# The products of probabilities and latents of a batch in one run, behind the value-output weights' product

## The chip, the cores and the metric

One core of a Trainium2 chip. The time is that of the device in microseconds, as the median of several executions. Engines: TensorE (PE, with its weight loads as PEld), VectorE (DVE), ScalarE (ACT), GpSimd (POOL), SyncE (SP), which here only issues transfers.

## What is computed

One layer on x of shape (2, 512, 512), all in fp32: latent attention with 32 heads, then a feed-forward part with low-rank corrections.

```python
def _mla_forward(hidden_states, Wq_a, q_a_ln_w, Wq_b, Wkv_a, kv_a_ln_w, Wkv_b, Wo):
    q = _rmsnorm(hidden_states @ Wq_a, q_a_ln_w) @ Wq_b        # rank 192, 32 heads of 128 + 64
    q_nope, q_pe = (q[..., :NOPE], q[..., NOPE:])
    ckv = hidden_states @ Wkv_a
    compressed, k_pe = (ckv[..., :KV_RANK], ckv[..., KV_RANK:])  # rank 64, rotary 64
    kv = _rmsnorm(compressed, kv_a_ln_w) @ Wkv_b
    k_nope, v = (kv[..., :NOPE], kv[..., NOPE:])
    ...  # rotary embedding of q_pe and k_pe
    scores = jnp.einsum('bhqd,bhkd->bhqk', qf, kf) * scale
    scores = jnp.where(causal, scores, jnp.finfo(scores.dtype).min)
    probs = jax.nn.softmax(scores, axis=-1)
    o = jnp.einsum('bhqk,bhkd->bhqd', probs, v)
    return o @ Wo

x = x + _layernorm(_L0_attn_ref(_layernorm(x)))
x = x + _layernorm(_L0_ffn_ref(_layernorm(x)))
```

## The kernel before

The kernel works with the latents themselves. It folds the key half of Wkv_b into the query weights, and the value half into Wo, so that a head's output is first probabilities times the 64 normalised latents, and later one product with the folded weights. Four stages follow each other: latents of all tokens (to about 45 us), the attention loop over 16 pairs of heads (to about 465 us), the output projection, and the feed-forward part. The change is in the attention loop.

One body of the loop serves one pair of heads, p, in 16 units k: k = 0 to 7 are the first batch (in counts, number 2p, the even one), k = 8 to 15 the second (number 2p + 1, the odd one); within a batch, k // 4 % 2 is the head and i = k % 4 the block of 128 query rows, which by the causal mask has i + 1 blocks of keys. So units have 128, 256, 384, 512 columns in turn. Body 0 and body 15 are written out (`first`, `last`), the 14 between are a loop. There are no planner and no priorities: the order of each engine's queue is the order of the source in its own `body`, and semaphore waits tie the queues together.

For one unit the work goes round the engines:
- TensorE, `scores`, two units ahead (in unit k it makes the scores of unit k + 2): three fp32r products into bank k % 2. It waits until VectorE has read the same bank two units before (`a.s_masked`, U - 1).
- VectorE, `mask_and_max`, also two units ahead: adds the mask, scales, takes the row extreme (line 635).
- ScalarE, `exponent`, two units ahead: exp and its sum (line 367).
- TensorE, `turn_p`, last in unit k: turns the probabilities of unit k (line 1002), after `a.exp_made`.
- ScalarE, `move_p`, first in unit k: copies them from the bank to `pt` (line 375).

Around this, TensorE's body has other work at fixed units, each ahead of that unit's `turn_p`:
- `absorb_query(p + 1)` at k = 0, the query weights of the next pair, into bank XB (5); it needs the transfer `sq`.
- `output(2p - 1, ...)` at k = 1, 2, 3: probabilities times latents of the odd batch of the pair before, for j = 0, then 1, then 2 and 3 (j is the block of keys; the columns are 512 - 128 j). `output(2p, ...)` at k = 9 (j = 0) and k = 10 (j = 1, 2, 3). Each j is two products, one per head, with 64 output columns, in the two column halves of the array (line 1014). They add up in bank 4 and wait until all eight units of their batch are in `pt`.
- `absorb_output(p)` at k = 8: the value-output weights of this pair, two products of 64 output columns and 512 columns (line 1032), into bank XB. ScalarE copies them to `vs` at its k = 9 (line 446), and SP stores them to device memory.
- `turn_r(2p - 1)` at k = 4 and `turn_r(2p)` at k = 11: the reciprocals of the sums, turned, into bank XB (line 1024). The second waits for ScalarE's copy of the weights (`a.wvo_moved`), since both use the bank. ScalarE copies them to `rsb` (`move_r`, line 383) at k = 5 and 12, and VectorE scales the output with them (`scale_o`, line 648) at k = 6 and 13.
- `query` at k = 5, 7, 13, 15: the rotated and absorbed queries, five fp32r products of 512 columns each, into banks 6 and 7. VectorE rotates them (`rotate_swapped`, `rotate_own`), GpSimd adds the halves, ScalarE rounds them (`query_hi`, line 357, at k = 2, 4, 10, 12), VectorE takes the rest (`query_lo`, line 625).

Bank XB thus serves, in turn, the query weights, the odd batch's reciprocals, the value-output weights and the even batch's reciprocals, and each user waits for the reader of the one before.

SP's loop for pair p: wait `wq_split`, load `sq`; wait `wvo_made`, load `sv`; wait `wvo_moved`, store `vs`. The load of `sq` of a pair stands behind the store of the pair before.

In body 15 there are no queries; at k = 11 to 15 pieces of the output projection (`project`) stand in their place, and ScalarE and VectorE split the folded weights.

Of the kernel before, what the change touches and what calls it, by code (L numbers as in the profile page):

```python
# [30 lines left out]
QB = SEQ // P  # L31
# [44 lines left out]
def build(nc, x_d, wa_d, lnw_d, cst_d, kcs_d, sq_d, sv_d, w13_d, bs_d, a13_d, a2_d, w2_d, b2_d, out_d):  # L76
# [137 lines left out]
    with block:  # L214
# [120 lines left out]
        def _(act):  # L335
# [80 lines left out]
            def body(p, first=False, last=False):  # L416
                for k in range(PU):
                    if last and k == 6:
                        split_output(0, 0)
                    if last and k in (13, 14):  # L420
                        if k == 13:
                            act.wait_ge(a.o_made, 2 * PAIRS - 1)
                        split_weights(k - 7)
                    move_p(PU * p + k, k, 2 * p - 1 + k // UNITS if k % UNITS == 0 and not first else None)
                    n = k + 2
                    if n < PU:
                        exponent(PU * p + n, n, first and n < 4, 2 * p if n == UNITS and not first else None)
                    elif not last:
                        exponent(PU * p + n, n - PU, False, 2 * p + 1 if n == PU else None)
                    if k == (3 if first else 1) and not last:  # L430
                        weights_hi(p + 1)
                    if k in (2, 4):
                        h = (k - 2) // 2
                        query_hi(4 * p + 2 + h, 1, h, None if first else PU * (p - 1) + UNITS + QB * (h + 1))
                    if k in (10, 12) and not last:
                        h = (k - 10) // 2
                        query_hi(4 * p + 4 + h, 0, h, PU * p + QB * (h + 1))
                    if k == 5 and not first:
                        move_r(2 * p - 1)
                    if k == 12:  # L440
                        move_r(2 * p, first)
                    if k == 9:
                        act.wait_ge(a.wvo_made, p + 1)
                        if not first:
                            act.wait_ge(a.wvo_out, 16 * p)
                        nc.scalar.activation(vs[:, :], bank[XB][:, :], ACT.Copy).then_inc(a.wvo_moved, 1)
# [149 lines left out]
        def _(dve):  # L596
# [83 lines left out]
            def body(p, first=False, last=False):  # L680
                for k in range(PU):
                    n = k + 2
                    if n < PU or not last:
                        mask_and_max(PU * p + n, n % PU)
                    if last and k == 7:
                        split_output(0, 0)
                    if last and k >= 8:
                        split_weights(k - 8)
                    if k == (4 if first else 2) and not last:
                        weights_lo(p + 1)  # L690

                    b, r, gi = (1, k, 4 * p + 2) if k < UNITS else (0, k - UNITS, 4 * p + 4)
                    if k < UNITS or not last:
                        if first and k in (1, 2):
                            rotate_swapped(gi + k - 1, k - 1)
                            if k == 1:
                                rotate_own(gi, 0)
                        elif first and k == 3:
                            rotate_own(gi + 1, 1)
                        elif r == 1:  # L700
                            rotate_swapped(gi + 1, 1)
                        elif r in (0, 2) and not (first and k == 0):
                            rotate_own(gi + r // 2, r // 2)
                        if r in (3, 5):
                            query_lo(gi + r // 2 - 1, b, r // 2 - 1)
                        if r == 7 and not last:
                            rotate_swapped(gi + 2, 0)
                    if k == 6 and not first:
                        scale_o(2 * p - 1, p - 1, 1)
                    if k == 13:  # L710
                        scale_o(2 * p, p, 0)
                    if k == 7:
                        invert(2 * p, 0, first)
                    if k == 15:
                        invert(2 * p + 1, 1)
# [242 lines left out]
        def _(pe):  # L958
# [17 lines left out]
            def query(gi, b, h, w=None, first=False):  # L976

                if w is not None:
                    pe.wait_ge(a.wq_split, w + 1)
                if not first:  # L980
                    pe.wait_ge(a.q_rotated, gi - 1)
                out, tok = bank[6 + h][:, :], slice(b * SEQ, (b + 1) * SEQ)
                three(out, w1_hi[:, h, :], w1_lo[:, h, :], ql_hi[:, 0, tok], ql_lo[:, 0, tok], True, False)
                nc.tensor.matmul(out, w2[:, h, :], ql_hi[:, 1, tok], start=False, stop=False)  # L984
                nc.tensor.matmul(out, w2[:, h, :], ql_lo[:, 1, tok], start=False, stop=True).then_inc(a.q_made, 1)  # L985
# [20 lines left out]
            def output(m, b, js, first=False):  # L1006

                if 0 in js:
                    pe.wait_ge(a.p_moved, UNITS * (m + 1))
                    if not first:  # L1010
                        pe.wait_ge(a.o_scaled, m)
                for j in js:
                    for h in range(2):
                        last = nc.tensor.matmul(bank[4][RKV * h:RKV * (h + 1), j * P:SEQ], kvn[:, QB * b + j, 0:RKV],  # L1014
                                                pt[:, b, h, j, j * P:SEQ], start=(j == 0), stop=(j == QB - 1),
                                                skip_group_check=True)
                if QB - 1 in js:
                    last.then_inc(a.o_made, 1)
# [34 lines left out]
            def body(p, first=False, last=False):  # L1053
                for k in range(PU):
                    n = k + 2
                    if n < PU:
                        scores(PU * p + n, n, 4 * p + n // QB)
                    elif not last:
                        scores(PU * p + n, n - PU, 4 * p + 4)
                    if k == (2 if first else 0) and not last:  # L1060
                        if first:
                            pe.wait_ge(f.qk_split, TB - 1)
                        else:
                            pe.wait_ge(a.r_moved, 2 * p - 1)
                        absorb_query(p + 1)
                    if k == 1 and not first:
                        output(2 * p - 1, 1, [0])
                    if k == 2 and not first:
                        output(2 * p - 1, 1, [1])
                    if k == 3 and not first:  # L1070
                        output(2 * p - 1, 1, [2, 3])
                    if k == 4 and not first:
                        if last:
                            pe.wait_ge(a.r_moved, 2 * p - 1)
                        else:
                            pe.wait_ge(a.wq_split, p + 2)
                        turn_r(2 * p - 1)
                    if k == 8:
                        if first:
                            pe.wait_ge(a.wq_split, p + 2)  # L1080
                        else:
                            pe.wait_ge(a.r_moved, 2 * p)
                        absorb_output(p)
                    if k in (5, 7) and not last:
                        query(4 * p + 4 + k // 7, 0, k // 7, p + 1)
                    if k == 9:
                        output(2 * p, 0, [0], first)
                    if k == 10:
                        output(2 * p, 0, [1, 2, 3])
                    if last and k in (11, 12, 13, 14, 15):  # L1090
                        project(0, 0, {11: (0,), 12: (1,), 13: (2,), 14: (3, 4), 15: (5,)}[k])
                    if k == 11:
                        pe.wait_ge(a.wvo_moved, p + 1)
                        turn_r(2 * p)
                    if k in (13, 15) and not last:
                        query(4 * p + 6 + k // 15, 1, k // 15)
                    turn_p(PU * p + k, k, first and k < 2)
                    if first and k < 2:
                        if k == 0:
                            pe.wait_ge(f.qk_split, TB)  # L1100
                        query(2 + k, 1, k)
# [211 lines left out]
```

## Time and profile before

| what | value |
|---|---|
| time, median of 3 (lowest, highest) | 654.0 us (653.73, 654.58) |
| profiled execution: span of the instructions | 652.1 us |
| the same execution's own time | not given apart; the median above is 1.9 us over the span |
| busy TensorE / VectorE / ScalarE / GpSimd | 607.9 / 529.2 / 412.8 / 166.0 us |
| granted TensorE clock, mean | 0.984 of full speed |

An engine's share is its busy time over the span. The end of a matmul is modelled, so on TensorE the distance from one start to the next says more than the duration of a row. A row `x3` merges three instructions; `[0.17 <-ACT pr L367]` says that the engine stood idle 0.17 us before it, until ScalarE's line 367 was done. In a row of fp32 products one product is two instructions.

### The profile page before, as it was taken

The page shows a single profiled execution, that of the slowest core. Times are in us where ns is not written, and L with a number is a line of the kernel's source. Part 1 is how long each engine was busy: PE and PEld are TensorE (multiplying, and loading weights), DVE is VectorE, ACT ScalarE, POOL GpSimd, SP SyncE. Part 2 cuts the span into 40 slices and gives each one's busy share as a digit, 9 for nine tenths or more (in the row PEclk, how much of TensorE's full clock was granted, in tenths as well). Part 3 has the DMA queues.
Part 4 walks back from the last instruction along what each step waited for, and adds up shares of the span by engine and source line. Part 5 has one row for each costly group of instructions (what it writes and reads, how often), then busy time and mean ns, then how long its engine had stood idle before and what let it go on. Part 6 is the DMA issues. An engine that isn't in the chain of part 4 may idle for free.

```text
span 652.1 us, 12397 instructions
## 1 busy us (share of the span) xinstructions
PE 607.9 (93%) x3432; PEld 448.6 (69%) x3432; DVE 529.2 (81%) x1292; ACT 412.8 (63%) x1157; POOL 166.0 (25%) x137
## 2 busy tenths in 40 slices
PE   5778999999999999999999999999999878789996
PEld 4666667767777776677677777766787656666664
DVE  4987788888888888888888888889877888886456
ACT  4455777878777777778787777777733333155343
POOL 2011222122213212221222132121043333125520
PEclk9998999999999999999999999999999998979999
DMA  8000211201202202112012022022760000001003
GB/s 320 16 1 1 82 39 43 80 25 56 80 0 80 65 15 80 36 44 80 19 61 80 0 80 64 17 93 80 234 235 1 0 1 1 28 2 49 0 16 114
DMA packets 13862, 37.80 MB, mean 58 GB/s; under 512 B 1328, under 2 KB 1584, under 8 KB 13584
## 3 DMA queue, kind: packets, MB, share of 16 engines
q1 hardware_dynamic: 13840, 37.53, 17.3%
q8 instruction: 11, 0.18, 0.1%
q14 instruction: 11, 0.09, 0.0%
HBM read 31.24 MB, written 6.29 MB: 58 GB/s over the span
## 4 chain that ended last, share of the span: by engine, by line
PE 71%; DVE 18%; ACT 4%; issue 3%; DMA 3%; SPq 0%; DVEq 0%; ACTq 0%
PE bank L1002 13%; PE bank L1014 12%; PE bank L961 11%; PE bank L962 11%; PE bank L963 11%; DVE dot L833 6%; PE bank L1032 2%; PE bank L1024 2%; PE bank L971 2%; PE bank L985 2%; PE bank L984 2%; DMA x<-x 2%; PE bank L1181 2%; DVE st L809 2%; DVE ss L635 1%
## 5 line engine op out<-in xcount | busy, mean ns | idle before, releaser
L367 ACT ACTIVATE pr<-ss,small 128x128 f32<-128x128 f32 (+3 forms) x256 | 143.2, 559 | 41.4 <-DVE small L635 40.8
L375 ACT ACTIVATE pt<-bank 128x128 f32<-128x128 f32 (+3 forms) x256 | 110.9, 433 | 61.3 <-PE bank L1002 61.1
L635 DVE CUSTOM_DVE_ANT_0 ss<-bank,cst 128x128 f32<-128x128 f32 (+3 forms) x256 | 123.3, 486 | 14.0 <-PE bank L963 9.6
L1002 PE MATMUL bank<-ident,pr 128*128 128x128 f32 x640 | 119.0, 284 | 3.1 <-ACT pr L367 2.9
L1002 PEld LDWEIGHTS bank<-ident,pr 128*128 128x128 f32 x640 | 75.6, 142 | 66.6 <-ACT pr L367 34.0
L284 POOL TENSOR_TENSOR qrot<-qrot,qswp 64x512 f32<-64x512 f32 x64 | 82.8, 1294 | 138.5 <-DVE qrot L621 138.5
L961 PE MATMUL bank<-kt_hi,qt_hi 128*128 128x128 f32 (+3 forms) x256 | 101.0, 394 | 3.6 <-DVE qt_lo L625 2.7
L1014 PE MATMUL bank<-pt,kvn 128*64 128x256 f32 (+3 forms) x512 | 86.2, 448 | 0.7 <-ACT pt L375 0.7
L963 PE MATMUL bank<-kt_hi,qt_lo 128*128 128x128 f32 (+3 forms) x256 | 83.2, 325 | 0.0
L962 PE MATMUL bank<-kt_lo,qt_hi 128*128 128x128 f32 (+3 forms) x256 | 83.0, 324 | 0.0
L625 DVE TENSOR_TENSOR qt_lo<-qrot,qt_hi 128x512 fp32r<-128x512 f32 x64 | 60.3, 942 | 24.7 <-ACT qt_hi L357 24.5
L294 POOL COPY rb<-small 128x512 f32<-128x512 f32 x32 | 19.8, 617 | 212.8 <-DVE small L643 212.8
L961 PE MATMUL bank<-wv,o_s 128*128 128x512 f32 x128 | 52.5, 410 | 10.0 <-POOL o_s L318 10.0
L961 PEld LDWEIGHTS bank<-kt_hi,qt_hi 128*128 128x128 f32 x256 | 49.9, 195 | 6.1 <-DVE qt_lo L625 2.9
L962 PE MATMUL bank<-wv,o_s 128*128 128x512 f32 x128 | 51.2, 400 | 0.0
L963 PE MATMUL bank<-wv,o_s 128*128 128x512 f32 x128 | 51.1, 399 | 0.0
L963 PEld LDWEIGHTS bank<-kt_hi,qt_lo 128*128 128x128 f32 x256 | 48.8, 191 | 2.7
L962 PEld LDWEIGHTS bank<-kt_lo,qt_hi 128*128 128x128 f32 x256 | 49.4, 193 | 0.1
L367 ACT ACTIVATION_READ_ACCUMULATOR pr<-ss,small 128x1 f32 x256 | 49.2, 192 | 0.0
L1014 PEld LDWEIGHTS bank<-pt,kvn 128*64 128x64 f32 x512 | 29.9, 135 | 27.8 <-ACT pt L375 11.6
L318 POOL TENSOR_TENSOR o_s<-ot,o_s 128x1024 fp32r<-128x1024 f32 x13 | 32.7, 2522 | 61.2 <-ACT o_s L397 61.2
L615 DVE TENSOR_TENSOR qswp<-bank,cst 32x512 f32<-32x512 f32 x64 | 44.5, 695 | 2.0
(168 smaller groups left out, 1179.7 us busy)
## 6 DMA issues: line engine op xcount, KB each, us to landing
sv<-sv SPq DMA_DIRECT2D x16, 576.0 KB, 3.7
sq<-sq SPq DMA_DIRECT2D x16, 448.0 KB, 3.5
wvo_scratch<-vs SPq DMA_DIRECT2D x16, 256.0 KB, 2.1
wv_raw<-wvo_scratch SPq DMA_DIRECT2D x8, 512.0 KB, 4.2
xa<-x SPq DMA_DIRECT2D x8, 256.0 KB, 5.5
x<-x SPq DMA_DIRECT2D x1, 2048.0 KB, 10.9
out<-yo SPq DMA_DIRECT2D x8, 256.0 KB, 2.0
w<-w SPq DMA_DIRECT2D x1, 1376.0 KB, 14.1
```

The source lines that it names most:

```text
L284: nc.gpsimd.tensor_tensor(qrot[RKV:P, h, :], qrot[RKV:P, h, :], qswp[RKV:P, h, :], ALU.add)\
L367: nc.scalar.activation(pr[:, k % 4, 0:n], ss[:, k % 2, 0:n], ACT.Exp, bias=negmax[:, k % 8:k % 8 + 1], scale=-1.0, accum_out=rsum[:, k:k + ...
L375: nc.scalar.activation(pt[:, b, h, 0:i + 1, i * P:(i + 1) * P], bank[2 + k % 2][:, 0:(i + 1) * P].rearrange("p (j q) -> p j q", q=P), ACT. ...
L615: nc.vector.tensor_tensor(qswp[64:96, h, :], G[96:128, :], sin1[96:128, :], ALU.mult)
L625: nc.vector.tensor_tensor(qt_lo[:, b, h, :], qrot[:, h, :], qt_hi[:, b, h, :].bitcast(F32), ALU.subtract)\
L635: nc.vector.tensor_tensor_reduce(out=ss[:, k % 2, 0:n], in0=bank[k % 2][:, 0:n], in1=mask[:, SEQ - n:SEQ], scale=-SCALE, scalar=3.4e38, op ...
L833: nc.vector.tensor_tensor_reduce(out=dot[:, j % 2, :], in0=xn2[:, :], in1=a13[:, j, :], scale=1.0, scalar=0.0, op0=ALU.mult, op1=ALU.add, ...
L961: nc.tensor.matmul(out, w_hi, x_hi, start=start, stop=False)
L962: nc.tensor.matmul(out, w_hi, x_lo, start=False, stop=False)
L963: return nc.tensor.matmul(out, w_lo, x_hi, start=False, stop=stop)
L1002: last = nc.tensor.transpose(bank[2 + k % 2][:, j * P:(j + 1) * P], pr[:, k % 4, j * P:(j + 1) * P], ident[:, :])
L1014: last = nc.tensor.matmul(bank[4][RKV * h:RKV * (h + 1), j * P:SEQ], kvn[:, QB * b + j, 0:RKV], pt[:, b, h, j, j * P:SEQ], start=(j == 0), ...
```

## The change

- The three pieces of `output` of the odd batch (k = 1, 2, 3) become one at k = 2.
- `absorb_output(p)` moves from k = 8 to k = 10, and right behind it all four j of `output(2p)` follow, so far at k = 9 and 10.
- `turn_r(2p)` moves from k = 11 to k = 12.
- ScalarE's copy of the value-output weights moves from k = 9 to k = 11, its copy of the even batch's reciprocals from k = 12 to k = 13; VectorE's scaling of that batch from k = 13 to k = 14.

Semaphores and their counts stay as they are.

```diff
@@ scalar engine, body @@
-                    if k == 12:
+                    if k == 13:
                         move_r(2 * p, first)
-                    if k == 9:
+                    if k == 11:
                         act.wait_ge(a.wvo_made, p + 1)
                         if not first:
                             act.wait_ge(a.wvo_out, 16 * p)
@@ vector engine, body @@
-                    if k == 13:
+                    if k == 14:
                         scale_o(2 * p, p, 0)
@@ tensor engine, body @@
-                    if k == 1 and not first:
-                        output(2 * p - 1, 1, [0])
                     if k == 2 and not first:
-                        output(2 * p - 1, 1, [1])
-                    if k == 3 and not first:
-                        output(2 * p - 1, 1, [2, 3])
+                        output(2 * p - 1, 1, range(QB))
...
-                    if k == 8:
+                    if k in (5, 7) and not last:
+                        query(4 * p + 4 + k // 7, 0, k // 7, p + 1)
+                    if k == 10:
                         if first:
                             pe.wait_ge(a.wq_split, p + 2)
                         else:
                             pe.wait_ge(a.r_moved, 2 * p)
                         absorb_output(p)
-                    if k in (5, 7) and not last:
-                        query(4 * p + 4 + k // 7, 0, k // 7, p + 1)
-                    if k == 9:
-                        output(2 * p, 0, [0], first)
-                    if k == 10:
-                        output(2 * p, 0, [1, 2, 3])
+                        output(2 * p, 0, range(QB), first)
...
-                    if k == 11:
+                    if k == 12:
                         pe.wait_ge(a.wvo_moved, p + 1)
                         turn_r(2 * p)
```

## Rows read from the trace of the kernel before

**Rows 1.** The page, part 1: busy us (share of the span) xinstructions.

```profile
PE 607.9 (93%) x3432; PEld 448.6 (69%) x3432; DVE 529.2 (81%) x1292; ACT 412.8 (63%) x1157; POOL 166.0 (25%) x137
```

**Rows 2.** Stretches: length; busy PE, PEld, DVE, ACT, POOL; granted clock; DMA share; GB/s.

```profile
44.00:80.00 36.00, 31.24 (x174) 24.36 (x174) 26.99 (x79) 22.11 (x68) 8.36 (x7) 0.91 0.12 38
...
257.56:283.22 25.66, 25.49 (x163) 18.53 (x162) 22.03 (x57) 19.60 (x59) 6.37 (x6) 1.00 0.17 51
```

**Rows 3.** Timeline, TensorE, that body: start us, us, engine, line, operation, count.

```profile
259.35 0.40 PE L962 MATMUL bank<-kt_lo,qt_hi 128*128 128x512 f32 x1
259.59 0.40 PE L963 MATMUL bank<-kt_hi,qt_lo 128*128 128x512 f32 x1
259.91 1.08 PE L1014 MATMUL bank<-pt,kvn 128*64 128x512 f32 x4
260.92 0.44 PE L1002 MATMUL bank<-ident,pr 128*128 128x128 f32 x2
...
268.37 0.55 PE L1002 MATMUL bank<-ident,pr 128*128 128x128 f32 x3 [0.17 <-ACT pr L367]
...
271.31 1.08 PE L1032 MATMUL bank<-sv 128*64 128x512 f32 x4
...
273.28 1.08 PE L1014 MATMUL bank<-pt,kvn 128*64 128x512 f32 x4
...
274.48 0.30 PE L961 MATMUL bank<-kt_hi,qt_hi 128*128 128x128 f32 x1
...
274.94 1.52 PE L1014 MATMUL bank<-pt,kvn 128*64 128x384 f32 x12
276.39 0.55 PE L1002 MATMUL bank<-ident,pr 128*128 128x128 f32 x3
...
277.14 0.60 PE L1024 MATMUL bank<-ident,rb 128*128 128x128 f32 x4
277.58 0.60 PE L1002 MATMUL bank<-ident,pr 128*128 128x128 f32 x4
277.93 0.43 PE L961 MATMUL bank<-kt_hi,qt_hi 128*128 128x384 f32 x1
...
278.58 0.47 PE L961 MATMUL bank<-kt_hi,qt_hi 128*128 128x512 f32 x1
...
283.22 0.42 PE L961 MATMUL bank<-kt_hi,qt_hi 128*128 128x384 f32 x1
```

**Rows 4.** Timeline of VectorE in the same body.

```profile
270.46 0.69 DVE L648 TENSOR_TENSOR ot<-bank,rsb 128x512 f32 x1 [0.69 <-ACT rsb L383]
...
273.17 0.56 DVE L635 CUSTOM_DVE_ANT_0 ss<-bank,cst 128x384 f32<-128x384 f32 x1
```

**Rows 5.** Timeline of ScalarE in the same body.

```profile
268.13 0.19 ACT L367 ACTIVATION_READ_ACCUMULATOR pr<-ss,small 128x1 f32 x1
...
275.75 0.59 ACT L446 ACTIVATE vs<-bank 128x512 f32<-128x512 f32 x1
276.98 0.49 ACT L375 ACTIVATE pt<-bank 128x384 f32<-128x384 f32 x1 [0.64 <-PE bank L1002]
277.36 0.39 ACT L367 ACTIVATE pr<-ss,small 128x128 f32<-128x128 f32 x1
...
277.75 0.62 ACT L357 ACTIVATE qt_hi<-qrot 128x512 fp32r<-128x512 f32 x1
278.27 0.59 ACT L375 ACTIVATE pt<-bank 128x512 f32<-128x512 f32 x1
278.75 0.50 ACT L367 ACTIVATE pr<-ss,small 128x256 f32<-128x256 f32 x1
```

**Rows 6.** Timeline of SP in the same body, and landing of the sq loads.

```profile
276.50 0.35 SPq L235 DMA_DIRECT2D wvo_scratch<-vs  x1
277.38 0.33 SPq L231 DMA_DIRECT2D sq<-sq  x1
...
DMA to landing us min/median/max: 3.2/3.5/5.8
```

## The prediction

> **What bounds the kernel now.** First the busy time by engine: TensorE 93% of the span, VectorE 81%, ScalarE 63% [rows 1]. Such shares are averages, so next one pair of heads by itself: a steady body of the loop lasts 25.66 us, TensorE is busy for 25.49 of it at full clock, VectorE for 22.03 and ScalarE for 19.60 [rows 2]. TensorE looks like the only bound, but VectorE has only 3.6 us in hand and ScalarE 6.1, and the three engines feed one another every second unit. So the third view is the timeline of TensorE, and the question in each row is whether it starts where the row before lets it or where another engine does. In this body nearly all starts are TensorE's own. The exception is turning the probabilities of unit 6, at 268.37, which waits for exp(6): ScalarE's read of its sum ends at 268.32 [rows 3, 5]. TensorE therefore runs just ahead of a VectorE and ScalarE chain that is nearly as long as its own. That makes it necessary to walk the change through all three queues instead of adding up TensorE's savings. I write unit k for one row block of a body, turn(k) for turning its probabilities, mask(k) for VectorE's pass over its scores.
>
> **What the change takes from TensorE.** The products with 64 output columns stand in six runs per body now: three for the odd batch (units 1, 2, 3), one for the value-output weights (unit 8), two for the even batch (units 9, 10). The run of one 512-column pair takes 1.01 us from its start to the next instruction (259.91 to 260.92), that of 384, 256 and 128 columns, 768 in all, 1.45 us (274.94 to 276.39) [rows 3]. So 256 more columns cost 0.44 us, 512 columns 0.88, and 0.13 us of each run is not columns: leaving the run. Entering costs some more: score products of 512 columns follow each other at 0.24 (259.35 to 259.59), and the run starts 0.32 after the last (259.91); so 0.08 us. A run costs about 0.21 us beyond its columns by this, 0.24 if leaving is 0.16 as I take below for the longest one; I take 0.24. After the change there are two runs, so TensorE has 4 x 0.24 = 0.96 us less to do per body.
>
> The Trainium skill (TensorEngine Tiling, section Tiling Modes, Key Properties) says that changing the tiling mode, not merely the tile, drains TensorE. The trace agrees that going in and out costs time that the columns don't. By that rule alone the change is a gain; the rival that takes it so is the first below.
>
> **First half of a body (odd batch), units 0 to 6.** Two runs fewer: -0.48 us for TensorE. But turn(6) already waits for exp(6), and this comes behind mask(6) [rows 3, 5]: TensorE's gain ends there unless VectorE and ScalarE move too. They gain a little (turn(1) now comes 1 us sooner, and ScalarE's copies behind it), and lose a little: VectorE's scaling of the even batch's output moves one unit later, past the mask of the next body's unit 0, and now waits for a copy that ScalarE makes a unit later, so mask(2) is late for scores(4), by my estimate some 0.3 us (half of one such scaling, 0.69 in rows 4). Bounds -0.5 and +0.4; I take 0, since the row is one of waiting already.
>
> **Second half, from turn(6).** Here the moves matter.
> 1. scores(12) may not start before mask(10), which reads the same bank, is done. mask(10) ends at 273.17 + 0.56 = 273.73, which is 5.36 us after turn(6) [rows 3, 4]. VectorE can't do it sooner: its work before it is the even-batch rotation of the next body, and ahead of that the scaling at 270.46, which had idled 0.69 us for ScalarE's copy of the reciprocals, which hangs on exp(6) like turn(6) itself. TensorE now reaches scores(12) at 274.48, 6.11 us after turn(6), so 0.75 us to spare. But 2 x 1.01 = 2.02 us of what keeps it busy until then, the weights' product at 271.31 and the first even-batch product at 273.28, moves behind scores(12). TensorE comes at 6.11 - 2.02 = 4.09 and waits until 5.36 + 0.07 (semaphore; ScalarE's to TensorE took 0.05, rows 3 and 5) = 5.43. Wait 1.3 us; scores(12) is 0.68 us earlier than now.
> 2. From scores(12) to turn(10) it is 1.91 us now (274.48 to 276.39) [rows 3]. Two groups of 512 columns are added inside the one run, 2 x 0.855 (0.88 by the slope, 0.85 if leaving costs 0.16, since 1.01 - 0.16 = 0.85): +1.71 us.
> 3. The turning of the reciprocals (unit 11 now, at 277.14; unit 12 then) may not overwrite its bank before ScalarE has copied the weights' product, and this copy moves from unit 9 to unit 11. In ScalarE's queue it stands behind moving turn(10) (0.59 after turn(10)'s start: 276.39 to 276.98), exp(12), the rounded query copy, moving turn(11) and exp(13). Their starts are 276.98, 277.36, 277.75, 278.27, 278.75, and the next thing starts 0.49 after the last: 279.24. That is 2.85 us after turn(10); the copy itself takes 0.59 (275.75), ends at +3.44, and with 0.05 TensorE goes on at +3.49 [rows 5]. What TensorE has to do until then: turn(10) and scores(13), 0.75 (276.39 to 277.14), turn(11), 0.35 (277.58 to 277.93), scores(14), 0.61 (277.93 to 278.58, less 0.04 that I give to turn(12), one block): 1.7 us [rows 3]. It waits 1.8 us. Then 0.44 for the reciprocals (277.14 to 277.58) and 0.04 for turn(12), and scores(15) starts at +3.97. Now it starts at 278.58 - 276.39 = +2.19. So +1.78 us. Behind the waiting instruction on TensorE stand turn(12), scores(15) and the query products; VectorE's mask(15) and ScalarE's moves wait for them. Without the query copy in ScalarE's way (if it got done sooner) the wait would be 1.3 us; that is its lower bound.
> 4. From scores(15) to the next body's scores(2) is 4.64 us (278.58 to 283.22) [rows 3], TensorE's own work; nothing in it changes but the place of ScalarE's copy of the reciprocals (unit 13), which still ends before the next body's query weights need the bank. I take 0.
>
> Sum per body: 0 - 0.68 + 1.71 + 1.78 = **+2.81 us**, a body of about 28.5 us. It holds 1.3 + 1.8 us of new waiting, against 0.96 us of TensorE work saved.
>
> SP's queue is moved too: the store of the weights' product follows ScalarE's copy (0.88 us ahead of the load of the query weights, 276.50 and 277.38), and these land 3.5 us later in the median [rows 6]. Copy end to landing is some 0.2 + 0.9 + 3.5 = 4.6 us; after that copy's end TensorE needs 0.5 + 4.64 + 0.6 = 5.7 us to where it uses them. About 1 us of cover is left; the slowest load (5.8) would cost 1.2 us in a body. Counted as nothing, kept for the upper end. The load of the value weights is issued when their product is done, a whole body ahead: nothing.
>
> **The whole.** Fourteen bodies are like this one: 14 x 2.81 = 39.3 us. Body 0 has only the second half, its VectorE has one scaling less and its TensorE ran slower before it [rows 2], so the mask wait may be smaller: +2 (1.5 to 2.8). In the last body products of the output projection at units 11 and 12 cover 1.4 us of the wait for the copy, and there are no queries: +1 (-0.5 to 2). Sum +42.3 us. On the profiled execution: span 652.1 to 694.4. Its time is not shown apart from its span; the three runs have the median 654.0, 1.9 us above it, and with that the forecast is 654.0 + 42.3 = **696.3 us**.
>
> **Rivals.**
> - TensorE stays the bound (the other side): the waits don't come, and the saving does: 14 x 0.96 + 0.5 + 1.0 = 15 us, 639. It decides if mask(10) comes 1.3 us sooner after turn(6) and the copy 1.8 us sooner. For it: TensorE's 25.49 of 25.66 us busy. Against it: both are in-order queues whose rows stand back to back, and the last is a copy behind five instructions, two of them waiting for TensorE's own turn(11) or turn(10).
> - Only the wait for the copy comes: VectorE, its masks being ready sooner, gets ahead, and scores(12) starts when TensorE arrives. Then +2.81 - 1.33 = 1.48 per body, 14 x 1.48 + 2 = 23 us: 677. Against: the 0.69 us that VectorE idled for ScalarE's copy.
> - The clock falls as well. In the stretch from 44 to 80 us, where TensorE was busy for 31.24 of 36.00, the granted clock was 0.91 against 1.00 in the steady bodies [rows 2]. A share of 0.18 of 36 us at the lower of the two levels (1.2 GHz) is 6.5 us, a loss of 3.2. Half of that per body would be 14 x 1.6 = 23 us more: 719. For it: TensorE would be busy for some 25.4 of 28.5 us, 0.89, little above the 0.87 there. Against: that stretch still begins in the first stage, whose waits are many, while here two waits of under 2 us lie some 6 us apart.
> - The change doesn't do what it says: the 0.24 us is not a cost of a run but of the first product after another kind, and stays. In the second half the waits hide it, so it shows only as some 0.25 us per body: 700.
>
> **Chances.** Forecast 0.72, TensorE stays the bound 0.05, copy wait alone 0.10, clock 0.08, no saving 0.05. The range: from the copy wait alone with a first half at its lower bound, (1.48 - 0.1) x 14 + 2 = 21, to the forecast with half of the clock's loss and late loads, +62: 674 to 716. Measured differences under 0.2% (1.3 us) count as the same: faster 0.06, same 0.02, slower 0.92.
>
> **What would show it.** In a steady body: two runs of 64-column products, the second 3.2 us long; TensorE idle 1.3 us before scores(12), put down to VectorE's mask, and 1.8 us before the turning of the reciprocals, put down to ScalarE's copy; bodies 28.5 us apart; VectorE's busy time per body unchanged at 22. Wrong, if bodies stand at 25.7 us or less, if the waits are there but at other places, or if the granted clock in the steady bodies is under 1.00.

## The result and the profile after

The changed kernel takes **695.0 us** (694.0 to 696.1), the kernel before 653.9 in the same comparison: a ratio of 1.063, 95% interval 1.061 to 1.066. The forecast was 696.3 us. The profiled execution took 694.56 us, its span is 692.8 us, 40.7 more than before.

The page, part 1, of the changed kernel, as in [rows 1]:

```profile
PE 605.9 (87%) x3432; PEld 456.9 (66%) x3432; DVE 523.8 (76%) x1292; ACT 410.4 (59%) x1157; POOL 165.5 (24%) x137
```

TensorE's busy time, whose ends are modelled, fell by 2.0 us while the span grew by 40.7: the time is waiting. One steady body, from turn(6) to the next turn(6) (length; busy PE, PEld, DVE, ACT, POOL; granted clock; DMA share; GB/s), against [rows 2]:

```profile
259.66:288.05 28.39, 25.38 (x160) 19.10 (x161) 21.63 (x56) 19.45 (x60) 6.35 (x6) 1.00 0.14 46
```

28.39 us in place of 25.66, TensorE busy for 25.38 of it, at full clock. The timeline of TensorE in it (start, duration, engine, line, operation, count, idle time before and what ended it), against [rows 3]:

```profile
259.66 0.55 PE L1002 MATMUL bank<-ident,pr 128*128 128x128 f32 x3 [0.16 <-ACT pr L367]
...
262.51 0.27 PE L1002 MATMUL bank<-ident,pr 128*128 128x128 f32 x1
262.84 0.50 PE L961 MATMUL bank<-kt_hi,qt_hi 128*128 128x512 f32 x1
...
263.63 0.38 PE L1002 MATMUL bank<-ident,pr 128*128 128x128 f32 x2
265.08 0.33 PE L961 MATMUL bank<-kt_hi,qt_hi 128*128 128x128 f32 x1 [1.07 <-DVE small L635]
...
265.56 1.08 PE L1032 MATMUL bank<-sv 128*64 128x512 f32 x4
266.47 2.33 PE L1014 MATMUL bank<-pt,kvn 128*64 128x512 f32 x16
268.73 0.55 PE L1002 MATMUL bank<-ident,pr 128*128 128x128 f32 x3
...
269.83 0.42 PE L961 MATMUL bank<-kt_hi,qt_hi 128*128 128x384 f32 x1
...
272.21 0.66 PE L1024 MATMUL bank<-ident,rb 128*128 128x128 f32 x4 [1.60 <-ACT vs L446]
...
272.73 0.48 PE L961 MATMUL bank<-kt_hi,qt_hi 128*128 128x512 f32 x1
...
277.36 0.42 PE L961 MATMUL bank<-kt_hi,qt_hi 128*128 128x384 f32 x1
...
279.63 0.38 PE L1002 MATMUL bank<-ident,pr 128*128 128x128 f32 x2
280.12 0.33 PE L961 MATMUL bank<-kt_hi,qt_hi 128*128 128x128 f32 x1
...
280.60 2.38 PE L1014 MATMUL bank<-pt,kvn 128*64 128x512 f32 x16
282.91 0.55 PE L1002 MATMUL bank<-ident,pr 128*128 128x128 f32 x3
...
288.05 0.55 PE L1002 MATMUL bank<-ident,pr 128*128 128x128 f32 x3 [0.17 <-ACT pr L367]
```

Two waits stand there that [rows 3] has not: 1.07 us before scores(12) (265.08), ended by VectorE's mask, and 1.60 us before the turning of the reciprocals (272.21), ended by ScalarE's copy into `vs`. The idle time named is counted from the modelled end of the row before; from start to start the waits are longer: turn(9), two blocks, begins at 263.63 and would be through at 263.77, so 1.31 us are lost. Counted like that, turn(6) waits 0.3 us as before, and there are short waits that carry no mark. The turning of one block ahead of scores(11) takes 0.33 us (262.51 to 262.84) where 0.03 to 0.08 is usual, and that of two blocks ahead of scores(4) takes 0.49 (279.63 to 280.12) where 0.14 is usual. Each of these two scores starts 0.06 to 0.07 us after the mask that reads its bank: mask(9) and mask(2) below. A shorter one, 0.1 to 0.2 us, stands before scores(7).

All in all TensorE waits some 4.3 us in this body, against some 0.5 in the body before. What is left, 24.1 us and 25.2, is also what bodies with two and with six runs take where TensorE waits for nothing (experiments 10 and 5). So the change did save 1.1 us of TensorE's work, where 0.96 was forecast.

What the waits hang on, first VectorE (mask(9), mask(10), and the scaling of the even batch behind mask(0) of the next body, with mask(2) after it), against [rows 4]:

```profile
262.36 0.41 DVE L635 CUSTOM_DVE_ANT_0 ss<-bank,cst 128x256 f32<-128x256 f32 x1
...
264.46 0.56 DVE L635 CUSTOM_DVE_ANT_0 ss<-bank,cst 128x384 f32<-128x384 f32 x1
...
275.63 0.29 DVE L635 CUSTOM_DVE_ANT_0 ss<-bank,cst 128x128 f32<-128x128 f32 x1 [0.44 <-PE bank L963]
...
276.79 0.69 DVE L648 TENSOR_TENSOR ot<-bank,rsb 128x512 f32 x1 [0.86 <-ACT rsb L383]
...
279.50 0.56 DVE L635 CUSTOM_DVE_ANT_0 ss<-bank,cst 128x384 f32<-128x384 f32 x1
```

then ScalarE, against [rows 5]:

```profile
269.31 0.49 ACT L375 ACTIVATE pt<-bank 128x384 f32<-128x384 f32 x1 [2.22 <-PE bank L1002]
269.69 0.39 ACT L367 ACTIVATE pr<-ss,small 128x128 f32<-128x128 f32 x1
...
270.08 0.62 ACT L357 ACTIVATE qt_hi<-qrot 128x512 fp32r<-128x512 f32 x1
270.60 0.58 ACT L375 ACTIVATE pt<-bank 128x512 f32<-128x512 f32 x1
271.08 0.50 ACT L367 ACTIVATE pr<-ss,small 128x256 f32<-128x256 f32 x1
...
271.57 0.59 ACT L446 ACTIVATE vs<-bank 128x512 f32<-128x512 f32 x1
```

The same five pieces stand ahead of the copy, with the same distances as in [rows 5] (0.38, 0.39, 0.52, 0.48, 0.49), and ScalarE idled 2.22 us before the first of them: it had nothing to do while TensorE was in the long run, and had everything to do after it.

### The profile page after: what moved, and what is told of

Read it like the earlier page. It is cut to its first block, busy times and chain, and to the rows that moved or that the text cites. A ratio compares the mean times of both kernels' runs of the same rounds, so it can differ in the third digit from the quotient of the medians.

```text
span 692.8 us, 12397 instructions
## 1 busy us (share of the span) xinstructions
PE 605.9 (87%) x3432; PEld 456.9 (66%) x3432; DVE 523.8 (76%) x1292; ACT 410.4 (59%) x1157; POOL 165.5 (24%) x137
## 4 chain that ended last, share of the span: by engine, by line
PE 53%; DVE 20%; issue 12%; ACT 10%; DMA 2%; DVEq 1%; SPq 0%; ACTq 0%
PE bank L1014 10%; PE bank L961 10%; PE bank L963 8%; PE bank L962 8%; PE bank L1002 6%; DVE dot L833 6%; ACT pr L367 3%; PE bank L1024 3%; PE bank L1032 2%; DVE ss L635 2%; ACT pt L375 2%; DMA x<-x 2%; DVE st L809 1%; PE bank L1174 1%; ACT rsb L383 1%
## 5 line engine op out<-in xcount | busy, mean ns | idle before, releaser
L1002 PE MATMUL bank<-ident,pr 128*128 128x128 f32 x640 | 115.6, 279 | 4.2 <-ACT pr L367 4.0
L1002 PEld LDWEIGHTS bank<-ident,pr 128*128 128x128 f32 x640 | 78.5, 142 | 26.6 <-ACT pr L367 8.0
L1014 PE MATMUL bank<-pt,kvn 128*64 128x256 f32 (+3 forms) x512 | 75.2, 436 | 0.7 <-ACT pt L375 0.7
L625 DVE TENSOR_TENSOR qt_lo<-qrot,qt_hi 128x512 fp32r<-128x512 f32 x64 | 57.7, 902 | 17.1 <-ACT qt_hi L357 17.1
L1014 PEld LDWEIGHTS bank<-pt,kvn 128*64 128x64 f32 x512 | 35.4, 137 | 45.5 <-issue 34.3
L961 PE MATMUL bank<-wv,o_s 128*128 128x512 f32 x128 | 53.8, 420 | 6.7 <-POOL o_s L318 6.7
L962 PE MATMUL bank<-wv,o_s 128*128 128x512 f32 x128 | 52.3, 408 | 0.0
L963 PE MATMUL bank<-wv,o_s 128*128 128x512 f32 x128 | 52.1, 407 | 0.0
```

The source lines that it names most:

```text
L625: nc.vector.tensor_tensor(qt_lo[:, b, h, :], qrot[:, h, :], qt_hi[:, b, h, :].bitcast(F32), ALU.subtract)\
L961: nc.tensor.matmul(out, w_hi, x_hi, start=start, stop=False)
L962: nc.tensor.matmul(out, w_hi, x_lo, start=False, stop=False)
L963: return nc.tensor.matmul(out, w_lo, x_hi, start=False, stop=stop)
L1002: last = nc.tensor.transpose(bank[2 + k % 2][:, j * P:(j + 1) * P], pr[:, k % 4, j * P:(j + 1) * P], ident[:, :])
```

## The experiments

All are timed beside the kernel before on the same chip; a body is measured from turn(6) to turn(6), or between two equal places, in the steady loop. In the diffs `...` stands for lines left out, and the comments after `#` are added here.

**1. The copy first in unit 10** (the run stays in unit 10).

```diff
+                    if k == 10:   # scalar engine, ahead of move_p(10)
+                        act.wait_ge(a.wvo_made, p + 1)
...
-                    if k == 11:
-                        act.wait_ge(a.wvo_made, p + 1)
```

> The changed kernel (695.0 us), with one edit: ScalarE copies the value-output weights' product first thing in unit 10, ahead of moving turn(10), not last in unit 11; everything else stays, so the single run is still at unit 10 behind scores(12). My theory: the 1.8 us per body in which TensorE waits for this copy go, since the copy is then ready before TensorE gets there, and nothing else is late in its place; TensorE's turning of the reciprocals comes 1.75 us sooner after turn(10), the wait before scores(12) stays at 1.1 to 1.3 us: 16 x 1.75 = 28 us less at most, about 669 us (665 to 674), steady body 26.6 us. Rival, that the copy wait only covers a chain of VectorE and ScalarE that is as long: less than half of it comes back, the time stays over 682 us.

667.2 us (ratio 1.021, 1.018 to 1.023): 27.8 us came back, as the theory had it, and the body is 26.57 us (turn(6) at 247.00 and 273.57). The wait before scores(12) stayed as it was, so the copy's wait was not cover for another:

```profile
247.00 0.55 PE L1002 MATMUL bank<-ident,pr 128*128 128x128 f32 x3 [0.16 <-ACT pr L367]
...
252.43 0.33 PE L961 MATMUL bank<-kt_hi,qt_hi 128*128 128x128 f32 x1 [1.06 <-DVE small L635]
...
273.57 0.55 PE L1002 MATMUL bank<-ident,pr 128*128 128x128 f32 x3 [0.17 <-ACT pr L367]
```

**2. The run in unit 9**, ahead of scores(12), copy and the rest late as in the changed kernel.

```diff
-                    if k == 10:
+                    if k == 9:
                         if first:
                             pe.wait_ge(a.wq_split, p + 2)
```

> The changed kernel (695.0 us), with one edit on TensorE: the run (weights' product and all products of the even batch) stands in unit 9, ahead of scores(12), not in unit 10 behind it. Copies, turning of reciprocals and scaling stay at their late units. My theory: the wait for mask(10) goes (TensorE is busy for 3.2 us while VectorE gets there), and the wait for the copy stays, 1.3 us or somewhat more: scores(15) at 11.7 us after turn(6) against 13.0 in the changed kernel, so 1.3 to 1.5 us per body less: about 674 us (669 to 679). Rival, that TensorE waits for VectorE's masks wherever the run stands: the wait moves to the next scores and the time stays over 688 us.

681.6 us (1.042, 1.040 to 1.045), outside the 669 to 679 expected; a body of 27.43 (turn(6) at 254.20 and 281.63): 0.96 us shorter than the changed kernel's, where I expected 1.3 to 1.5. The mask wait of 1.31 us is gone as expected; the miss is ScalarE. The run now stands ahead of turn(9) and not behind it, so ScalarE has one unit more to make up for when it ends, exp(11) of 512 columns among it. TensorE's turn(11) waits for that, 0.34 us from start to start, which is the difference between 1.31 and 0.96; and then the copy's wait is as long as before. This is read from the trace; no run moved exp(11) by itself:

```profile
285.70 1.08 PE L1032 MATMUL bank<-sv 128*64 128x512 f32 x4
...
290.48 0.66 PE L1002 MATMUL bank<-ident,pr 128*128 128x128 f32 x4 [0.17 <-ACT pr L367]
...
293.22 0.66 PE L1024 MATMUL bank<-ident,rb 128*128 128x128 f32 x4 [1.57 <-ACT vs L446]
```

**3. Both repairs, the reciprocals at their old units.** The run in unit 9, the copy first in unit 9, `turn_r`, `move_r`, `scale_o` of the even batch at 11, 12, 13.

```diff
-                    if k == 11:   # scalar engine: the copy; now ahead of move_p(9)
+                    if k == 9:
...
-                    if k == 10:   # tensor engine: absorb_output and output
+                    if k == 9:
...
-                    if k == 12:   # turn_r; move_r 13 -> 12, scale_o 14 -> 13
+                    if k == 11:
```

> Both repairs together: one run in unit 9, ScalarE's copy of the weights' product first thing in unit 9, and the turning of the reciprocals, their copy and the scaling at the units of the kernel before (11, 12, 13); the odd batch's products in one run in unit 2 as in the changed kernel. My theory: no new wait is left and the four runs saved are worth what TensorE can use of them, -0.3 to -0.9 us per body against the kernel before: 640 to 650 us, most likely 647. Rival 1, that the waits were not the cause but the long run itself: over 660 us. Rival 2, that entering and leaving a run costs nothing: 653 to 655 us.

646.0 us (0.989, 0.987 to 0.991): 1% faster than the kernel before, within the range of 640 to 650. The two long waits were the cause of the loss, and the long run by itself is not.

**4. The odd batch alone**, the kernel before with one run in unit 2.

```diff
-                    if k == 1 and not first:
-                        output(2 * p - 1, 1, [0])
                     if k == 2 and not first:
-                        output(2 * p - 1, 1, [1])
-                    if k == 3 and not first:
-                        output(2 * p - 1, 1, [2, 3])
+                        output(2 * p - 1, 1, range(QB))
```

> The kernel before (653.9 us), with only the first part of the change: the odd batch's three pieces in one run in unit 2; all of the even batch as before. TensorE has 2 x 0.24 us less to do per body. My theory: turn(6) waits for exp(6) on the VectorE and ScalarE chain, so most of it ends there, 0 to -0.15 us per body: 651.5 to 654 us. Rival, that TensorE alone bounds the body: -0.48 x 15 = -7 us, 647 us. If the moved work makes a new wait for VectorE in the first half it is slower, 655 to 658 us.

644.4 us (0.986, 0.984 to 0.989). Outside all that I had written: -9 us, more than the 7 us that I gave to TensorE's saving of two runs, and better than experiment 3 with four runs saved. The body went from 25.66 to 25.03, all of it before turn(6). VectorE's remainder of the query weights shows why; the kernel before, then this one:

```profile
263.25 0.29 DVE L604 TENSOR_TENSOR w_lo<-bank,w_hi 128x128 fp32r<-128x128 f32 x1 [0.54 <-ACT w L351]
```

```profile
257.00 0.08 DVE L635 DVE_READ_ACCUMULATOR2_ANT small<- 128x1 f32 x1
257.00 0.28 DVE L604 TENSOR_TENSOR w_lo<-bank,w_hi 128x128 fp32r<-128x128 f32 x1
```

In the kernel before VectorE idles 0.54 us for ScalarE's rounding of these weights, which stood behind moving turn(1), and turn(1) behind the first piece of the odd batch. With unit 1 short, the idle time is gone. Whether that or the saved runs are worth the 9 us is the question of experiment 5.

**5. The odd batch's three pieces, each one unit later.** No run is saved, unit 1 is short.

```diff
-                    if k == 1 and not first:
+                    if k == 2 and not first:
                         output(2 * p - 1, 1, [0])
-                    if k == 2 and not first:
+                    if k == 3 and not first:
                         output(2 * p - 1, 1, [1])
-                    if k == 3 and not first:
+                    if k == 4 and not first:
                         output(2 * p - 1, 1, [2, 3])
```

> The kernel before (653.5 us beside the last runs), with the odd batch's three pieces kept apart but each one unit later: j = 0 in unit 2, 1 in unit 3, 2 and 3 in unit 4. No run is saved, only unit 1 is short. Two readings of why one run in unit 2 gave 9 us where I expected 2 at most. (a) The chain: turn(1) comes 1.0 us sooner, ScalarE's move behind it, its exp(3) and the rounding of the query weights too, and VectorE no longer idles 0.54 us for them, so mask(6), exp(6) and turn(6) come sooner: then this kernel gains nearly as much, -0.45 to -0.6 us per body, 645 to 647 us. (b) The saved entering and leaving of two runs, 0.48 us: then this kernel gains nothing, 653 to 655 us.

646.1 us (0.989, 0.987 to 0.991), a body of 25.17 (278.87 - 253.70, the query weights' products). So 7.2 of the 9 us come without a single run saved. The odd part's gain is mainly the place, not the count. In this body TensorE waits for nothing, turn(6) included, and is the bound; in number 4, with two runs less to do, it meets the chain of VectorE and ScalarE again (turn(6) waits 0.3 us), so that only 0.14 us per body of what the two runs save is left.

```profile
253.70:278.87 25.17, 25.17 (x161) 18.47 (x161) 21.80 (x57) 19.60 (x60) 6.34 (x6) 1.00 0.17 52
```

```profile
253.70 1.00 PE L971 MATMUL bank<-sq 128*128 128x64 f32 x8
...
255.95 1.08 PE L1014 MATMUL bank<-pt,kvn 128*64 128x512 f32 x4
...
257.80 0.87 PE L1014 MATMUL bank<-pt,kvn 128*64 128x384 f32 x4
...
259.70 0.87 PE L1014 MATMUL bank<-pt,kvn 128*64 128x256 f32 x8
...
278.87 1.00 PE L971 MATMUL bank<-sq 128*128 128x64 f32 x8
```

**6. Copy early, reciprocals at their old units, the run still in unit 10.**

```diff
-                    if k == 12:   # turn_r; move_r 13 -> 12, scale_o 14 -> 13
+                    if k == 11:
```

> The kernel with the copy first in unit 10 (667.2 us), and the turning of the reciprocals, their copy and the scaling put back from units 12, 13, 14 to 11, 12, 13. The single run still stands in unit 10 behind scores(12). It prices the late units by themselves: from turn(6) to turn(6) the first half of a body took 10.18 us with the odd batch in one run and all else as before, but 10.69 in the changed kernel, and I put the 0.5 us to VectorE's scaling, which now stands behind mask(0) of the next body and waits for a later copy. Theory: 0.5 us per body less, 659 us (657 to 661), a steady body of 26.05 us, of which the wait before scores(12) still costs. Rival: the late scaling is free, 666 to 668 us.

659.4 us (1.009, 1.007 to 1.012), body:

```profile
269.54:295.60 26.06, 24.78 (x160) 19.13 (x161) 21.82 (x56) 19.31 (x60) 6.35 (x6) 1.00 0.15 50
```

26.06, as forecast: the late units cost 0.51 us per body. All of it lies between scores(2) and the next turn(6), 10.18 us here and 10.69 with the late units, and the wait before scores(4) is gone. Between this kernel and number 3 only the place of the run and of the copy with it differ, in front of scores(12) or behind it: 13.3 us, 1.0 per body. So of the 3.34 us per body between the changed kernel and number 3 the copy's place is 1.82, the late units are 0.51, and the run's place, with the copy kept ahead of the work behind it, is 1.01.

**7. The even batch's part alone.**

```diff
+                    if k == 1 and not first:
+                        output(2 * p - 1, 1, [0])
                     if k == 2 and not first:
-                        output(2 * p - 1, 1, range(QB))
+                        output(2 * p - 1, 1, [1])
+                    if k == 3 and not first:
+                        output(2 * p - 1, 1, [2, 3])
```

> The changed kernel (695.0 us) with the odd batch's pieces back in units 1, 2 and 3: the even batch's part of the change alone. If the parts add up, it loses what the odd part gave alone, 0.6 us per body: 704 us (702 to 707), a steady body of 29.0 us. Rival: the odd part's gain is void in the changed kernel, since the late units set the first half there anyway: 694 to 697 us.

697.0 us (1.067, 1.064 to 1.070), a body of 28.53 (turn(6) at 261.00 and 289.53). My theory of 702 to 707 us was wrong and the rival was right: what the odd batch's run gives alone, 9 us, is worth 2 here. The parts don't add up.

**8. Only the even batch's products in one run** in unit 10, the weights' product left in unit 8.

```diff
-                    if k == 9:
-                        output(2 * p, 0, [0], first)
                     if k == 10:
-                        output(2 * p, 0, [1, 2, 3])
+                        output(2 * p, 0, range(QB), first)
```

> The kernel before (653.5 us), with the even batch's products (not the weights' product) in one run in unit 10 behind scores(12); the weights' product stays in unit 8 and all copies where they were. One run less, 0.24 us. Theory: TensorE reaches scores(12) 1.01 us sooner, had 0.75 to spare, so it waits some 0.3 us for mask(10), and after it has 0.86 us more to do: +0.1 to +0.2 us per body, 655 to 657 us. Rival, only TensorE's work counts: -0.24 x 16 = -4 us, 650 us.

655.1 us (1.0024, 1.0012 to 1.0036): +0.18 us per body, body 25.84. One run less and slower, by a wait of the forecast kind. scores(12) starts 5.42 us after turn(6), as in the changed kernel and as forecast there; from start to start some 0.4 us are lost before it, where I expected 0.3:

```profile
243.34 0.55 PE L1002 MATMUL bank<-ident,pr 128*128 128x128 f32 x3 [0.17 <-ACT pr L367]
...
248.76 0.33 PE L961 MATMUL bank<-kt_hi,qt_hi 128*128 128x128 f32 x1 [0.23 <-DVE small L635]
...
269.18 0.55 PE L1002 MATMUL bank<-ident,pr 128*128 128x128 f32 x3 [0.18 <-ACT pr L367]
```

**9 and 10. VectorE's first query remainder behind mask(6)**, in kernels 4 and 3.

```diff
-                        if r in (3, 5):
-                            query_lo(gi + r // 2 - 1, b, r // 2 - 1)
+                        if r in (4, 5):
+                            query_lo(gi + r - 4, b, r - 4)
```

> The kernel with only the odd batch in one run (644.4 us), and VectorE's two query_lo per batch moved from units 3 and 5 (11 and 13) to 4 and 5 (12 and 13), so behind mask(6) (mask(14)). In the trace the first of them takes 1.66 us and not 0.69, since it starts while GpSimd adds the rotated halves, and mask(6), exp(6) and turn(6) stand behind it. Theory: the chain of VectorE and ScalarE sets the body (25.03 us), so with mask(6) 1.6 us sooner TensorE no longer waits for exp(6) (0.17 us named, some 0.3 in start to start): -0.3 to -0.4 us per body, 639 us (637 to 642). Rival: another place of the chain is as late, nothing changes, 643 to 646 us.

> The same move of query_lo in the kernel with two runs and both repairs (646.0 us), where the four saved runs gave nothing over the odd part alone. Theory: what TensorE saved in the second half was lost in front of turn(6) and turn(15), which waited for the chain; with a shorter chain the saved 0.48 us of that half count, so this kernel is now the faster of the two: 634 us (631 to 638), a body of 24.4 us. Rival 1: entering and leaving costs nothing that can be had in the second half, this one is level with the other, within 2 us. Rival 2: the chain behind the long run in unit 9 sets the second half, and it stays over 641 us.

638.4 us (0.977, 0.975 to 0.979) and **631.2 us** (0.966, 0.965 to 0.968), the fastest of all. Both lie within what was expected (637 to 642, and 631 to 638 at its very edge: the body is 24.08 us where I expected 24.4). The remainder in kernel 4, in the way of mask(6):

```profile
259.18 1.66 DVE L625 TENSOR_TENSOR qt_lo<-qrot,qt_hi 128x512 fp32r<-128x512 f32 x1
260.76 0.54 DVE L635 CUSTOM_DVE_ANT_0 ss<-bank,cst 128x384 f32<-128x384 f32 x1
```

One body of number 9 and one of number 10:

```profile
249.81:274.48 24.67, 24.67 (x162) 18.75 (x162) 21.26 (x57) 19.46 (x60) 6.34 (x6) 1.00 0.17 53
```

```profile
246.17:270.25 24.08, 24.08 (x162) 18.91 (x162) 21.17 (x57) 19.13 (x60) 6.37 (x6) 1.00 0.17 54
```

In both TensorE is busy for the whole body, 24.67 of 24.67 and 24.08 of 24.08: now it is the bound, and now the two runs that number 10 has less count: 0.59 us, 0.30 each. No short wait hides under the modelled ends: apart from the rows right before and right behind a run, those of the two bodies follow each other at the same distances from start to start, to 0.02 us. Number 5, bound by TensorE too, has two runs more than number 9 and takes 0.50 us more, 0.25 each. So six, four and two runs make 25.17, 24.67 and 24.08 us, with TensorE the bound each time.

In kernels 4 and 3, where turn(6) still waits for exp(6), the same two runs gave nothing (25.03 and 25.05). From start to start TensorE waits 0.4 us in number 4 and 1.0 in number 3: besides turn(6), 0.3 us before scores(11), which has mask(9) ahead of it as in the changed kernel, and 0.1 to 0.2 before scores(7) and scores(2).

## Why the prediction was right, point by point

- **The body**: forecast about 28.5 us, measured 28.39. Fourteen times the 2.73 more is 38.2 of the 40.7 us of span; 2.5 are left for the first and last body, forecast 3. The second run is 3.17 us long (265.56 to 268.73), forecast 3.2; VectorE is busy for 21.63 us of the body, forecast 22. Both waits stand where they were forecast.
- **Step 1**: scores(12) 5.43 us after turn(6), measured 265.08 - 259.66 = 5.42. The trace puts the wait down to VectorE's mask. That it comes from putting the run behind scores(12) is shown by experiment 2, in which only the run is moved and this wait goes, by 3 against 6, and, at a third of the size, by 8. No run made mask(10) itself come sooner.
- **Step 2**: turn(10) 1.91 + 1.71 = 3.62 after scores(12), measured 3.65.
- **Step 3**: the reciprocals 3.49 after turn(10), measured 3.48; scores(15) at +3.97, measured 4.00. Experiment 1 took the wait away and gave 27.8 us, 1.82 in the body; the forecast for it had been 28 at most.
- **Step 4**: 4.64, measured 277.36 - 272.73 = 4.63. SP's queue: no wait for the query weights' load shows in the body, as counted.
- **First half**: forecast 0, measured 10.69 against 25.66 - 14.85 = 10.81, so -0.12. The size was right, the reason was not. "TensorE's gain ends there unless VectorE and ScalarE move too" was true, but I took their moving for small. They gain 0.5 to 0.6 us from the short unit 1 (experiments 5 and 4), and lose 0.5 in this kernel to the late scaling (experiment 6). The wait for mask(2) itself, estimated at 0.3 us, came: 0.35 before scores(4). So the loss was nearly priced, the gain was not, and a term of 0 is right because the two cancel: that is luck. Had I priced the odd part alone, I would have been wrong; I was, in the expectation for experiment 4. Experiment 7 says the two are one chain: with the late units in place the gain is void.
- **TensorE's saving** of 0.24 per run: 0.25 to 0.30 measured where TensorE is the bound (5, 9 and 10). Between 9 and 10, entering is 0.10 of it, leaving 0.15, and 0.05 is a term that the forecast lacks: the turning behind a run takes longer (0.19 us for two blocks, 0.14 elsewhere). The rival that this cost stays falls with it. The rival of TensorE as the bound in the changed kernel falls by the two waits. The Trainium skill (TensorEngine Tiling, Tiling Modes, Key Properties) says that changing the tiling mode drains TensorE. The trace agrees that the change costs time, and that, on the way in, it is the half array and not the fp32 product that does: in the kernel before, the same score product of 384 columns takes 0.18 us ahead of the fp32 products from `sq`, which use the whole array, and 0.27 ahead of those from `sv`, which use half of it (rows below). What the engine does in that time no row shows.
- The sum by that saving alone, 639 us, came out nowhere by that reasoning: with the run, the copy and the reciprocals in place the time is 646.0 (3), and only the move of VectorE's remainder brings it to 631.2 (10).
- **The range**: the measured 695.0 lies in it, but its ends don't follow from the terms. The lower end takes 0.1 us for the first half where the bound named is 0.5, which would give 670 and not 674; the late loads in the upper end have no price of their own.
- **The copy wait alone** (677): not so, the mask wait came too. **The clock**: 1.00 in the body in spite of the two waits (1.31 us, and 272.21 - 269.83 - 0.61 = 1.77 us from start to start).

The rows on the array's two uses, from the kernel before (the run from `sv` follows the last one, at 271.31 in [rows 3]):

```profile
257.98 0.34 PE L963 MATMUL bank<-kt_hi,qt_lo 128*128 128x384 f32 x1
258.16 1.00 PE L971 MATMUL bank<-sq 128*128 128x64 f32 x8
...
271.04 0.34 PE L963 MATMUL bank<-kt_hi,qt_lo 128*128 128x384 f32 x1
```

No experiment was made on why the query remainder takes 1.66 us in place of 0.69, but the traces tell when it does. In kernel 4 it ends 0.56 us after GpSimd's addition of the rotated halves does; in number 10 it starts later against that addition, takes 1.18 us, and ends 0.56 us after it again:

```profile
259.00 1.28 POOL L284 TENSOR_TENSOR qrot<-qrot,qswp 64x512 f32<-64x512 f32 x1 [3.07 <-DVE qrot L621]
```

```profile
276.71 1.29 POOL L284 TENSOR_TENSOR qrot<-qrot,qswp 64x512 f32<-64x512 f32 x1 [3.04 <-DVE qrot L621]
```

```profile
277.38 1.18 DVE L625 TENSOR_TENSOR qt_lo<-qrot,qt_hi 128x512 fp32r<-128x512 f32 x1
```

The Trainium skill (SBUF — State Buffer, Who interferes with whom) says that a VectorE tensor_tensor with both inputs in SBUF contends with GpSimd's reads, and that the later of the two is held until the first is through. The traces agree in the main. In the loops of all the kernels here, every remainder that starts within 1.03 us of the addition's start ends 0.54 to 0.56 us after the addition, whenever it started: starting 0.18, 0.67, 0.95 or 1.02 us after the addition's start, it takes 1.66, 1.17, 0.90 or 0.81 us. One that starts 1.2 us after it (numbers 5 and 8), or meets none, takes 0.69. The 0.55 us that are left behind the addition are less than 0.69, so not all of the remainder is held. A mask of 256 columns, which has one of its inputs in a bank, takes 0.42 us inside an addition (277.53 in the kernel before) as it does outside of one (282.58). No run took the addition away with all else in place; that it lengthens the remainder is shown, why it does is argued.

## What to carry to other kernels

Merging pieces saves their entering and leaving, here 0.25 to 0.30 us each, but the pieces were also the time in which the other engines caught up: before moving one, write down for each instruction it jumps over what that waits for and how much slack it had (here 0.75 us against 2.02 moved). A copy that frees a bank belongs right behind its producer in the reader's queue, not behind work that waits for later work of the producer. A saving on the busiest engine counts only once the chain through the others is shorter: take the parts one by one, since the gain and the loss of one change may sit in different parts of it.

## What the runs showed of the hardware that was not expected

The subtraction just named: 0.69 us by itself, up to 1.66 beside GpSimd's addition. The place of this one instruction per batch was worth 6.1 us (kernel 4 to 9) and 14.8 us (kernel 3 to 10). The move does two things at once, it takes the instruction out of mask(6)'s way and shortens it to about 1.17 us, and no run tells them apart.
